# The last batch's tail split into two chains by halves of the tokens, and scale and shift folded into an eviction

## The reference

```
x_comb  = concat(x_global, x_local)
x_fused = silu(x_comb @ fus_w1.T + fus_b1) @ fus_w2.T + fus_b2
x = layer_norm(x + x_fused, gn_g, gn_b)
x_ffn = silu(x @ ffn_w1.T + ffn_b1) @ ffn_w2.T + ffn_b2
x = layer_norm(x + x_ffn, fn_g, fn_b);  t = t + x
n = _ln_t(t);  logits = n @ gate_w + gate_b;  idx = argmax(softmax(logits))
pos = cumsum(one_hot(idx)) of the token, over all batches   # the slot in the expert's buffer
```

## Time and profile before

| | us |
|---|---|
| median of 3 runs | 1966.23 |
| lowest, highest | 1964.11, 1969.98 |
| the profiled execution | 1971.81 |
| its span, first to last instruction | 1969.2 |
| busy: PE, DVE, ACT, POOL | 1616.7, 1334.0, 1031.5, 715.0 |

### The profile page before, as it was taken

The page is one execution under the profiler, slowest core; times in us unless marked ns, Lnnn a source line. Parts: engine busy times, 40 slices in busy tenths (PEclk is TensorE's granted clock), DMA queues, the critical chain, the costliest instruction groups (busy, mean ns, idle before and its releaser), DMA issues.

```text
span 1969.2 us, 24543 instructions
## 1 busy us (share of the span) xinstructions
PE 1616.7 (82%) x8264; PEld 759.1 (39%) x8264; DVE 1334.0 (68%) x2698; ACT 1031.5 (52%) x1970; POOL 715.0 (36%) x1113
## 2 busy tenths in 40 slices
PE   5758889998998898979898996889788886339993
PEld 2513322533443253325433442344223322227772
DVE  4258868797789768976897697869698821116660
ACT  1311566477656655665575665656564663223431
POOL 3101301245215530553154315421453441436883
PEclk7765899999999899989998998999898968559995
DMA  5281241335053405241533244132414110023346
GB/s 169 73 152 45 81 102 48 80 128 117 19 125 98 95 13 135 94 95 28 155 95 59 44 141 103 38 44 97 106 66 87 44 38 2 1 81 74 74 55 184
DMA packets 125921, 161.66 MB, mean 82 GB/s; under 512 B 19116, under 2 KB 86449, under 8 KB 125798
## 3 DMA queue, kind: packets, MB, share of 16 engines
q1 hardware_dynamic: 109926, 148.61, 29.6%
q0 software_dynamic: 13568, 7.31, 2.8%
q10 hardware_dynamic: 2304, 4.20, 0.6%
HBM read 103.36 MB, written 58.52 MB: 82 GB/s over the span
## 4 chain that ended last, share of the span: by engine, by line
PE 45%; DVE 18%; POOL 11%; DMA 9%; ACT 7%; SPq 6%; issue 5%; POOLq 0%; DVEq 0%; ACTq 0%
PE bank L1280 8%; PE bank L1249 7%; PE bank L1268 7%; DVE gmax L1728 7%; POOL t_d L1117 6%; PE bank L1206 6%; PE bank L1317 3%; PE bank L1307 3%; PE bank L1127 2%; SPq L891 2%; ACT prob L1523 2%; DVE cmax L1666 2%; DMA k_stack<-parts_d 2%; DMA kv_d<-lqkv 2%; DMA q_stack<-gneg_rows 2%
## 5 line engine op out<-in xcount | busy, mean ns | idle before, releaser
L1523 ACT ACTIVATE prob<-bank 128x512 f32<-128x512 f32 x1024 | 573.4, 596 | 348.8 <-PE bank L1268 346.9
L1728 DVE TENSOR_REDUCE gmax<-bank 128x1 f32<-128x512 f32 x1024 | 653.9, 681 | 65.9 <-PE bank L1249 65.0
L1268 PE MATMUL bank<-q_stack,k_stack 99*128 99x512 bf16 x1024 | 390.4, 397 | 71.1 <-ACT prob L1523 33.8
L1249 PE MATMUL bank<-k_stack,q_stack 96*128 96x512 bf16 x1024 | 402.9, 402 | 55.8 <-DVE gmax L1728 27.5
L1280 PE MATMUL bank<-prob,v_tok 128*32 128x512 f32 x2048 | 282.7, 626 | 2.1 <-ACT prob L1523 2.1
L1062 POOL TENSOR_TENSOR lprod<-ql_tok,kv_win 128x640 f32<-128x640 f32 x64 | 102.2, 1618 | 371.1 <-DMA ql_tok<-ql_d 347.1
L1249 PEld LDWEIGHTS bank<-k_stack,q_stack 96*128 96x128 bf16 x1024 | 101.4, 99 | 316.1 <-DVE gmax L1728 206.3
L1268 PEld LDWEIGHTS bank<-q_stack,k_stack 99*128 99x128 bf16 x1024 | 100.4, 100 | 249.0 <-ACT prob L1523 158.4
L1069 POOL TENSOR_TENSOR lprod<-ls,kv_win 128x640 f32<-128x640 f32 x64 | 80.8, 1284 | 227.5 <-DVE ls L1783 227.1
L1027 POOL TENSOR_TENSOR mv<-stats 128x4 f32<-128x4 f32 x64 | 13.0, 203 | 393.5 <-DVE stats L1700 393.5
L1117 POOL DMA_INDIRECT t_d<-kv_win,token_e x80 | 130.0, 1625 | 53.1 <-DVE kv_win L1928 29.0
(11 more groups left out here) (215 smaller groups left out, 2458.3 us busy)
## 6 DMA issues: line engine op xcount, KB each, us to landing
kv_win<-kv_d SPq DMA_DIRECT2D x32, 1280.0 KB, 5.6
parts_d<-parts SPq DMA_DIRECT2D x16, 768.0 KB, 3.6
q_stack<-parts_d SPq DMA_DIRECT2D x96, 128.0 KB, 6.9
k_stack<-parts_d SPq DMA_DIRECT2D x96, 128.0 KB, 7.4
kv_d<-lqkv SPq DMA_DIRECT2D x64, 128.0 KB, 2.5
rows_d<-rows SPq DMA_DIRECT2D x10, 528.0 KB
cprob<-rows_d SPq DMA_DIRECT2D x8, 660.0 KB, 4.7
x_cm<-in_x_dram SPq DMA_DIRECT2D x8, 512.0 KB, 3.5
```

What stands on the lines that cost most here:

```text
L1249: mm(max_ps[max_bank(n)][:, :], q_stack[quad][0:KROWS, h, i * P:(i + 1) * P], k_stack[quad][0:KROWS, h, j * HN:(j + 1) * HN], start=True, ...
L1268: mm(score_ps[n % 2][:, :], k_stack[quad][0:KM, h, j * P:(j + 1) * P], q_stack[quad][0:KM, h, half * HN:(half + 1) * HN], start=True, stop ...
L1523: nc.scalar.activation(prob[:, g % 2, h, :], score_ps[n % 2][:, :], ACT.Exp).then_inc(exp_made, 1)
L1728: v.tensor_reduce(gmax[:, h, i, j:j + 1], max_ps[max_bank(n)][:, :], AX.X, ALU.max)\
```

## The change

The last batch (`B - 1`) no longer goes through `tail_a` and `tail_b`. For each half a chain `end_of_half` runs from `o_tokens` to `route`, with two banks of its own (banks 1, 2 and banks 3, 0, free by then), own semaphores, own tanh and half tiles (in `cprob`), and routing by halves (4 running sums and 4 indirect DMAs each). In these chains

- `fuse1` takes the local product (`flT`) first, and the local `o_channels` come before the global ones;
- ACT makes only the tanh; the scaled copy goes to DVE, behind the tanh;
- mean and variance come from `bn_stats` and `bn_aggr` on DVE; POOL makes only the power -0.5; the normalisations are DVE instructions (`tensor_scalar` with mean and rstd; for `norm_v` two `scalar_tensor_tensor`, one of them before the rstd is there);
- POOL does `affine_u` (a_old = x1 * gn_g + (gn_b + ffn_b2)) beside the chain.

In all batches `x1` stays without scale and shift; the eviction `x1_channels` on ACT applies them per partition from `gn_cols`, which two more weight loads fill. POOL now has 2 instead of 3 wide operations in `norm_u` and in `norm_v`, per half; `bias` has a second one over all 1024 tokens (t_old + fn_b). The scheduler's costs change with it, and so do the orders of all batches from batch 1 on.

```diff
-    "bias": [("pool", 2.4, 0.2)],
+    "bias": [("pool", 4.9, 0.2)],
-    "norm_u": [("act", 1.6, 0.1), ("pool", 4.0, 0.1)],
-    "norm_v": [("act", 1.6, 0.1), ("pool", 4.0, 0.1)],
+    "norm_u": [("act", 1.6, 0.1)],
+    "affine_u": [("pool", 2.6, 0.1)],
+    "norm_v": [("act", 1.6, 0.1), ("pool", 2.6, 0.1)],
...
+END_BANKS = [(1, 2), (3, 0)]
...
+def end_of_half(s, a, h):
+    chain, ps = f"end{h}", (f"end{h}", 2)
...
+    add("o_tokens", 0, ps=ps, before=[(a, ("o_copy", 0, h)), (a, ("guard_rows", 1)), (a, ("local_qkv", NT - 1))])
+    add("o_channels", 1, ps=ps, before=[(a, ("local_out", NT // 2 - 1)), (a - 1, ("logits",))])
+    add("o_tokens", 1, ps=ps, before=[(a, ("o_copy", 1, h))])
...
+    add("norm_t2", before=[done("stats", 2), (a - 1, ("route",))])
+    add("n2_channels", ps=ps, before=[done("norm_t2")])
+    add("logits", ps=ps, before=[done("n2_channels")])
+    add("ranks", ps=ps, before=[done("logits")] + ([(a, ("end_ranks", 0))] if h else []))
+    add("route", before=[done("ranks")])
...
-    tail_a(s, B - 1)
-    tail_b(s, B - 1)
+    for h in range(2):
+        end_of_half(s, B - 1, h)
...
+            loads += [(gn_cols[:, k:k + 1], v.rearrange("(c a) -> c a", a=1)) for k, v in enumerate((gn_g, gn_b))]
...
+            def affine_u(b, h):
                 t = slice(HT * h, HT * h + HT)
                 after(pool, normed, b * 6 + h + 1)
...
+                pool.tensor_tensor(a_old[:, t, :], x1[:, t, :], wide(BC["gn_g"]), ALU.mult).then_inc(affine_step, 1)
...
+            def end_stats(b, h, k):
+                pool.wait_ge(end_var[h], k + 1)
+                pool.tensor_tensor(rstd2[:, h, :], end_mv[h][:, :, 1], half_pow[:, :], ALU.pow).then_inc(end_rstd[h], 1)
...
             def x1_channels(b, h):
                 tail_wait(b, ("x1_channels", h))
-                to(y_cm[:, 0, h * HN:(h + 1) * HN], tail_ps[:, :]).then_inc(tail_free, 1)
+                to(y_cm[:, 0, h * HN:(h + 1) * HN], tail_ps[:, :], scale=gn_cols[:, 0:1], bias=gn_cols[:, 1:2])\
+                    .then_inc(tail_free, 1)
...
+            def end_silu(h, use, m, bias, n):
...
+                end_read_once(dve, h, use, m)
+                v.tensor_scalar(end_half[h][m], ps[:, :], 0.5, bias, ALU.mult, ALU.add).then_inc(free, 1)
...
+            def end_normalise(h, k, dst):
+                dve.wait_ge(end_rstd[h], k + 1)
+                for i in range(HT):
+                    last = v.tensor_scalar(dst[:, i, 0:C], x1[:, HT * h + i, :], end_mv[h][:, i, 0:1],
+                                           rstd2[:, h, i:i + 1], ALU.subtract, ALU.mult)
+                return last
```

More of the change, by code:

```diff
@@ L110 @@
 TAIL_TURN = {u: n for n, u in enumerate(TAIL_USES)}
+TAIL_COUNT = (B - 1) * (len(TAIL_USES) + 2) + 2
+END_USES = [("o_tokens", 0), ("o_channels", 1), ("o_tokens", 1), ("o_channels", 0), ("fuse1", 0), ("fuse1", 1),
+            ("fuse2",), ("x1_channels",), ("ffn1", 0), ("ffn1", 1), ("ffn2",), ("n2_channels",), ("logits",),
+            ("ranks",)]
+END_TURN = {u: n for n, u in enumerate(END_USES)}
+END_READERS = [2 if u[0] in ("fuse1", "ffn1") else 1 for u in END_USES]
+END_BANKS = [(1, 2), (3, 0)]
 TAIL_TURNS = len(TAIL_USES)
@@ L381, in normed @@
                   *([(a - 1, ("route",))] if name == "t2" else []))
+            if name == "u":
+                s.add("tail", a, ("affine_u", h), (a, ("norm_u", h)))
     for h in range(2):
@@ L389, in tail_b @@
         hidden("ffn1", h, (a, ("x1_channels", h)))
-        s.add("tail", a, ("ffn2", h), (a, ("ffn1", 1, h)), banks=TAIL_PS)
+        s.add("tail", a, ("ffn2", h), (a, ("ffn1", 1, h)), (a, ("affine_u", h)), banks=TAIL_PS)
     normed("v", "ffn2")
@@ new lines, in end_fuse1, with end_second @@
+            def end_fuse1(b, h, m):
+                ps, full = end_fill(h, "fuse1", m)
+                end_done(pe, h, "o_channels", 1)
+                mm(ps[:, :], flT[:, m * C:(m + 1) * C], y_cm[:, 1, h * HN:(h + 1) * HN], start=True, stop=False)
+                end_done(pe, h, "o_channels", 0)
+                mm(ps[:, :], fgT[:, m * C:(m + 1) * C], y_cm[:, 0, h * HN:(h + 1) * HN], start=False, stop=True)\
+                    .then_inc(full, 1)
+            def end_second(h, use, w, count):
+                ps, full = end_fill(h, use)
+                pe.wait_ge(end_hid[h], count)
+                for i in range(HT):
+                    t = HT * h + i
+                    for k in range(2):
+                        last = mm(ps[:, i * C:(i + 1) * C], hid[:, k, t * P:(t + 1) * P], w[:, k, :],
+                                  start=(k == 0), stop=(k == 1))
+                last.then_inc(full, 1)
@@ new lines, in end_fuse2, with end_x1_channels, end_ffn1 @@
+            def end_fuse2(b, h):
+                end_second(h, "fuse2", f2T, 2)
+            def end_x1_channels(b, h):
+                ps, full = end_fill(h, "x1_channels")
+                pe.wait_ge(end_normed[h], 1)
+                for i in range(HT):
+                    last = turn(ps[:, i * P:(i + 1) * P], x1[:, HT * h + i, :])
+                last.then_inc(full, 1)
+            def end_ffn1(b, h, m):
+                ps, full = end_fill(h, "ffn1", m)
+                end_done(pe, h, "x1_channels")
+                mm(ps[:, :], n1T[:, m * C:(m + 1) * C], y_cm[:, 0, h * HN:(h + 1) * HN],
+                   start=True, stop=True).then_inc(full, 1)
@@ L1366, in _ @@
                           ffn2=ffn2, n2_channels=n2_channels, logits=logits, ranks=ranks))
-            after(pe, tail_free, B * (TAIL_TURNS + 2))
+            after(pe, tail_free, TAIL_COUNT)
+            for h in range(2):
+                for use in END_USES[-2:]:
+                    end_done(pe, h, *use)
             def expert_columns(e):
```

321 lines of the change are left out of this document (300 added, 21 removed).

## The result

The change takes **1934.58 us** (median of 4 runs, 1932.41 to 1936.08). The kernel before, in the same comparison, took 1966.23 (median of 3, 1964.11 to 1969.98); a fourth execution of it, of 7463.07 us, is left out. The ratio is **0.9836, 95% interval 0.9805 to 0.9867**: faster by 32 us, where 49 were forecast, and 1.6 us above the top of the range. (A 95% interval says how far the ratio could lie from the truth by the scatter of the runs.) The profiled execution took 1934.97 us, its span is 1933.1.

What follows compares the result with a forecast made beforehand. From last scores to first expert no engine is full; a latency-bound chain of hand-overs bounds it. Terms +1 +7 -58 +0, with 1 given back, made -49: 1922.8 profiled, 1917 median, range 1901 to 1933.

Steps and rivals of the forecast that it cites:

- Start: Kernel start: two more column loads ahead of SP's other work cost +1.0 us, bounds +0.5 and +3.
- Score loop: Last batch, o_copy(1, 0) to o_copy(1, 1): half 0's chain between score tiles lengthens it by 7 us, bounds +3 and +12.
- rival 2: Score loop stalls: half 0's late returns to PE hold up score tiles, 14 us, giving 1931; chance 0.17.
- Half 1's chain: Last batch, o_copy(1, 1) to the expert rows: 64.5 us instead of 122.6, so -58.
- Rival 1: The clock stays up because two woven chains keep PE busier: 57.2 instead of 64.5, giving 1908; chance 0.13.
- the woven piece: Front of half 1's chain, with half 0's steps between: full clock in part of it, half clock from fuse2 on.
- Batches 0 to 6: Batches before the last: changed POOL work and new engine orders cost 0 in the mean, ±8 us.
- The sign that I had named: Start of batch 7's scores moved by more than 8 us either way would point to rivals 4 or 5.
- Rival 4: New orders put guard rows beside window loads: 9 us more in each of 6 batches, 54, giving 1971; chance 0.03.
- Rival 3: Overlap doesn't happen, both halves run together behind the last scores: gain only some 25 us, 1941; chance 0.04.
- The port: DVE instructions with two SBUF inputs block against POOL: at most 1.26 us a meeting, taken as 0.

Runs made afterwards that it cites:

- frozen order: Order of the kernel before, copied into the change for every step but the last batch's tail, as in e3 (ratio 0.9715) and e6 (0.9738).
- e6: The same kernel as e3, unaltered, run beside e5 on one chip: 1917.45 us, ratio 0.9738.
- e3: The change with the order of the kernel before for every step but the last batch's tail: 1930.84 us, ratio 0.9715.
- e2: The kernel before with scale and shift folded into the eviction and the second bias operation, order and costs of before: 1980.59 us, ratio 0.9962.
- e1: The kernel before, work untouched, with the change's scheduler costs for bias, norm_u and norm_v: 2007.72 us, ratio 1.0082.
- e4: e2's work under the change's scheduler costs and steps, last batch's tail not split: 2000.56 us, ratio 1.0063.
- e5: The change itself, unaltered, run beside e6 on one chip: 1935.40 us, ratio 0.9831.
- e11: The kernel before with only the scheduler's POOL cost of norm_v at 3.9 instead of 4.0: 1988.59 us, ratio 1.0021.
- e12: The kernel before with only the scheduler's DVE cost of logits at 1.85 instead of 1.75: 1993.49 us, ratio 1.0063.
- e15: The change with only the scheduler's POOL cost of norm_v back at 4.0 instead of 2.6: 1930.05 us, ratio 0.9802.
- e14: The change with the scheduler's costs of bias, affine_u and norm_v at the values of before: 1914.47 us, ratio 0.9727.
- e9: e3's kernel with half 0's chain from fuse1 on moved behind the last scores, in turn with half 1's: 1926.53 us, ratio 0.9718.
- e10: e3's kernel with PE waiting until a half's other bank is read too, in effect one bank per half: 1932.79 us, ratio 0.9764.
- e7: e6 with the steps behind the last scores placed, half 1's first power ahead of half 0's indirect DMAs: 1909.63 us, ratio 0.9700.
- e13: e7 with the last batch's bias ahead of batch 6's eight indirect DMAs on POOL: 1909.42 us, ratio 0.9693.

## Why the prediction was right and where it failed

*Start* (+1.0): 1.7, within its bounds.

*Score loop* (+7): +6.1, 32.3 us. The 32.0 without the local half's transposes was the better figure, since these run at 1616.53, ahead of the loop. The longest wait of PE in it was 0.9 us, for exp, so rival 2 did not come about. In the frozen order the loop takes 36 to 38: batch 6's ranks and the local half's eight transposes fall into it too (PE busy 29.5 us in e6, 27.4 here), and PE waits 2.4 us for DVE instead of 0.8. The term was right for the order that the change has.

*Half 1's chain* (64.5): 66.4, of which the meeting with the four indirect DMAs took 2.4. Rival 1, the clock up, did not happen: PE was at half speed from the second piece on (fuse1's product with flT at 1662.63 takes 1.92, its 1.13 at 1629.40 in the loop), earlier than the full-clock part that I had counted for the woven piece. e6 had the same steps in 62.0 us, with PE busy 21.7 us in them against 26.9 in the change, so the clock can account for all of the 4.4 between the stretches. It isn't the order alone that sets it: e3, the same kernel as e6, took 64.0, with PE busy 24.1. The four aggregates took 0.38 (0.7 to 0.85 taken) and the four normalisations 1.11 (0.95 taken).

*Batches 0 to 6* ("the orders of all engines change from batch 1 on ... I take 0, with ±8"): **this is the step that failed**. They came 12.1 us later, and nearly all of the miss between the profiled executions (1922.8 forecast, 1934.97 measured) is here: -49 + 12.1 = -37. The sign that I had named for such a miss, batch 7's scores more than 8 us off, was there: o_copy(1, 1) of batch 6 came 13.5 us later. The median missed by more, 17.6 us (1917 against 1934.58), since I took off the 5.6 us by which the one profiled execution of before lay above its median, and for the change that distance is 0.4. No row showed that it would repeat; without it the time would still be above the forecast by 12. The price of 0 for the work is borne out so far as e2 goes: POOL's fewer operations and the folded eviction did not cost anything (the whole kernel gained 7.5 us). It was wrong for the order, which cost 16 (e1), 20 (e4 against e2) and 18 us (e5 against e6). The ±8 was taken from how far single landings vary. It treated a new plan as symmetric about the old one. Six plans in which nothing but figures or the planner's steps changed the middle (e1, e4, e11, e12, e15 and the change) came out slower than the same work in the old order (e11 by 4 us, within its interval of nothing), and e14 alone was level. None was faster. Why the old order is the better one isn't shown; that it was kept because it measured well would explain it. A new order has a place in the sum of its own, and here that place was a cost.

*Rival 4* (the new orders cost 54 us by landings behind which PE stands) was right that the new orders cost, and wrong in the wait and the size: the landings rose by 4 us, the waits for DVE's maxima by 8.7. It stays open which steps of the order make these waits longer.

*Rival 3* priced a missing overlap at 24 us (1941 against 1917). e9 shows none (0.9718 against 0.9715 and 0.9738). I had worked out the loop and the chain as separate terms, and never set the +7 of the loop against what the chain would be with two halves in turn: 72 us, not the 95 that 1941 implies. So in these orders the gain of the change comes from the fold, the split on own banks and the DVE norms together; the shares of the last two weren't measured apart, but for the second bank (e10). Whether the overlap pays once the end's order is put right isn't shown: e7 stands at 0.9700 and e9 at 0.9718, with intervals that overlap, and no run has e9's order improved by hand.

*The port* (0 taken, at most 1.26 a meeting): the meeting came, in the loop, and it cost more. DVE and POOL of the change:

```profile
1632.52 2.35 POOL L1198 TENSOR_TENSOR t_old<-t_old,fnb_bc 128x1024 f32<-128x1024 f32 x1
1633.09 2.34 DVE L2175 SCALAR_TENSOR_TENSOR hid<-cprob 128x512 f32<-128x512 f32 x1
...
1636.12 0.69 DVE L2175 SCALAR_TENSOR_TENSOR hid<-cprob 128x512 f32<-128x512 f32 x1
```

hid on DVE, with both operands in SBUF, took 2.34 us instead of 0.69 while POOL worked through the 1024-wide bias operation, which the change itself adds. The 1.65 us more are within the 1.78 that were left of the POOL operation when hid began, and hid ended 0.56 us behind it. This agrees with the lock in the Trainium skill (SBUF — State Buffer, Who interferes with whom); my bound had used the 512-wide operations. It cost nothing in the end: fuse2 of half 0 starts 8.36 us behind fuse1 (1629.40 to 1637.76), and just so in e6 (1609.77 to 1618.13), where hid took 0.69.

## What to carry to other kernels

When a change also touches a planner's costs or steps, price the new order as a term of its own (on the slow side, if the old order was kept for its time), and test it by running the old work in the new order and the new work in the old one; here the order took back 18 of the 50 us that the rest of the change gave. Before giving an overlap a price, write down the two stretches on either side of it: here 9.5 us of PE work put under the score loop made it 9.9 us longer, since PE waited little in it. On a chain of hand-overs, look at each queue for what a late helper (here four indirect DMAs ahead of a 1 us power) has in front of it; moving these and half 0's last steps by hand gave 8 us for a few lines (in the profiles 6.7, of which 1.5 were a luckier clock).

## What the runs showed of the hardware that was not expected

- The eviction with scale and bias per partition took 0.78 us (1685.27) where the plain one of the same 128x512 takes 0.60, more than the 0.69 of an activation with a bias column.
- Four bn_aggr of 128x6 took 0.38 us together, less than half of the four bn_stats of 128x128 (0.87).
- The granted clock of the same instructions in the same place differs between executions, even of one kernel: ffn2 of half 1 took 3.75 us in e3 (clock 0.50) and 3.55 in e6 (0.54), the same program, and 3.75 in e13 (0.50) and 2.02 in e7 (1.00), which have one order there.
- A DVE instruction with two SBUF operands was held up by a POOL instruction to its end: hid took 2.34 us in the change and 2.65 in e5, the same kernel, instead of 0.69, and ended both times 0.56 us behind the POOL operation beside it.
